# A vision-tower kernel on one core: dense FFN for all tokens one to two groups behind the load, chosen rows written by an indirect store

## The chip, the cores and the metric

The kernel runs on one NeuronCore of a Trainium2 chip. Its time is the device time in microseconds of one execution. Five engines work beside each other, each in the order of its own instruction list, and wait for each other through semaphores: TensorE (PE, with its weight loads PEld), VectorE (DVE), ScalarE (ACT), GpSimd (POOL) and SyncE (SP), which here only issues DMAs.

## The reference, cut to what matters

The input is 64 images of 12 channels and 224 x 224 pixels; the output is 64 x 196 tokens of 192 values.

```python
# tokens: sums over 16x16 patches, then a 12 -> 192 projection
pooled = x.reshape(B, 12, 14, 16, 14, 16).sum(axis=(3, 5))
h = einsum('bcij,ce->bije', pooled, channel_weights).reshape(B, 196, 192)
# attention on xn = layernorm(h): 12 heads of 16, causal softmax over 196 tokens
attn_output = ctx @ out_w + out_b
selection = softmax((xn @ sel_w + sel_b) / temperature)[..., 1:]
idx = top_k(selection[..., 0], 14)            # 14 of 196 tokens of each image
y = xn with (attn_output * selection) added in the rows idx
h = h + y
# FFN: 192 -> 768 with exact gelu -> 192
h = h + gelu(layernorm(h) @ in_weight.T + in_bias) @ out_weight
```

Only the 14 chosen tokens of an image get an attention output. All other tokens are a function of 12 channel sums and two rsqrt scales, so their layer norms and the first FFN layer can be computed from 13 numbers per token.

## The kernel before

**Tiling.** Images are worked on in 16 groups (NG) of 4 (GB). The input of a group comes in 7 tiles (XT) of 1344 KB into four buffers X. GpSimd adds row pairs of a tile (line 364, in place), VectorE reduces the rest (line 828, `sum_tile`) into R. When a group's seven tiles are done, SyncE stores R to a scratch in HBM (line 334) and reads it back in another layout (Praw, line 341), GpSimd adds the quarters (`sum_quarters`, lines 376 to 382) and so has P, the 48 channel sums x 196 tokens.

**Stages of a group.** A (tokens): TensorE multiplies P by TMR (`tm`, line 445), giving moments and features F; VectorE gets the variance and, by an integer guess and three Newton steps, its rsqrt (`rsqrt`, lines 831 to 851, one call a period for all norms: ln1 of one group, ln2 of another, the chosen rows' of a third). z is transposed (`zt`, line 451) to FM; the selection goes through an exponential and a top-14 search (`top`) on 4 rows, and `slots` builds the one-hot Sg, `keep` (not chosen) and ST, a one-hot that spreads the 56 chosen rows of a group over its 784 tokens (line 939). K (stacks): the 13 numbers of each token are split in bf16 parts (SP; H, M, L on ScalarE, d1, d2 on VectorE) and transposed (`tr1`, `tr2`) to Stk1 for the first FFN layer and Stk2 for the residual; `keep` zeroes the chosen tokens. G and S: the attention of the 56 chosen rows (SLOTS), two heads side by side (112 rows, six pairs): U (line 493), scores (508), maximum (988), six exponentials (647), twelve transposes to ET (514), context (520) with ET stationary and F moving, GN (996) normalised, transposed back (`gt`, 526), G2, output `at` (531), h1. C: the chosen rows' own layer norm and FFN (XH, `f1` line 546, actS, `f2` line 551) to OS. F1: dense first layer, twelve bf16 matmuls (line 560) through one PSUM bank psF, each followed by a gelu on ScalarE (line 669). F2: seven output tiles of 112 tokens, each six f32 products with W2 (line 573; the trace has two records for one f32 matmul), one with the residual stack (577) and one that adds the chosen rows by ST (581), then a copy to obuf (677) and one store of the group.

**Order.** Each engine runs a body per period p; every stage has a lag: A works on group p-1, attention on p-2 and p-3, stacks on p-2, F1 on p-3, F2 on p-4. The body of TensorE has 24 slots (lines 585 to 605): `AT_F1` names the slots with a first-layer matmul and `IN_F2` how many of the 56 matmuls of F2 follow in each, so that F1's wait for gelu and the waits for VectorE have output tiles of an older group beside them. ScalarE has the matching list (line 684) and VectorE an explicit one (line 1042) in which the seven tile reductions L0 to L6 are spread:

```python
plan = ["S gt 3", "C os 4", "L 0", "S at 3", "G ga 2", "L 1", "L 2", "G u 2", "L 3", "L 4", "A var 1", "R", "A z 1",
        "C xh 3", "S sc 2", "A sel 1", "K v 2", "L 5", "A top 1", "K d1 2", "L 6", "A slots 1", "S g 2", "K d2 2",
        "A var2 1"]
```

SyncE issues the load of a tile's buffer when VectorE has reduced the tile four earlier. All weights are loaded by SyncE (lines 304 to 324) between the first input tiles, and their products are built on VectorE and TensorE (`weights`, `prepare`) during the first two periods; TensorE enters its periods after that.

## Time and profile before

| | |
|---|---|
| median of 3 runs | 1011.47 us (1010.99 to 1015.18) |
| span of the profiled execution | 1015.8 us |
| TensorE busy | 851.5 us, 84%; its weight loads 727.0 us |
| VectorE busy | 603.5 us, 59% |
| ScalarE busy | 309.6 us, 30%; 96 exponentials of 446 ns |
| GpSimd busy | 366.9 us, 36%; 112 halvings of 3035 ns |
| tile reductions on VectorE | 112 of 1540 ns |
| mean granted TensorE clock | 0.840 of full speed |
| HBM | 159 MB read, 12 MB written, 168 GB/s over the span |
| dense store of a group | 588 KB, 9.0 us from issue to landing |
| sums to HBM, sums back | 147 KB each, 4.4 and 4.5 us |

A duration is that of one instruction or of a run of like ones. A line with a bracket tells how long the engine had been idle and what released it. The granted clock has two levels here, 1.00 (2.4 GHz) and 0.50 (1.2 GHz); numbers between are a window with both.

### The profile page before, as it was taken

The page shows a single profiled execution, that of the slowest core. Times are in us where ns is not written, and L with a number is a line of the kernel's source. Part 1 is how long each engine was busy: PE and PEld are TensorE (multiplying, and loading weights), DVE is VectorE, ACT ScalarE, POOL GpSimd, SP SyncE. Part 2 cuts the span into 40 slices and gives each one's busy share as a digit, 9 for nine tenths or more (in the row PEclk, how much of TensorE's full clock was granted, in tenths as well). Part 3 has the DMA queues.
Part 4 walks back from the last instruction along what each step waited for, and adds up shares of the span by engine and source line. Part 5 has one row for each costly group of instructions (what it writes and reads, how often), then busy time and mean ns, then how long its engine had stood idle before and what let it go on. Part 6 is the DMA issues. An engine that isn't in the chain of part 4 may idle for free.

```text
span 1015.8 us, 14313 instructions
## 1 busy us (share of the span) xinstructions
PE 851.5 (84%) x4772; PEld 727.0 (72%) x4772; DVE 603.5 (59%) x1305; ACT 309.6 (30%) x736; POOL 366.9 (36%) x164
## 2 busy tenths in 40 slices
PE   0550436499889999998989999999999999999998
PEld 0530334488678878887878888787888788889887
DVE  1769787856687777575665667474756555243200
ACT  0000023323234343333342424133333334253520
POOL 3484544434352626262624334262626240000000
PEclk9955555579899999796969789797979597999999
DMA  9674935444555565554646444455546441000000
GB/s 258 274 282 163 349 121 217 163 145 189 193 217 199 217 206 212 200 217 147 272 145 245 161 159 181 145 216 201 219 155 262 145 164 37 1 25 1 24 25 24
DMA packets 23901, 172.11 MB, mean 169 GB/s; under 512 B 3144, under 2 KB 6408, under 8 KB 9482
## 3 DMA queue, kind: packets, MB, share of 16 engines
q1 hardware_dynamic: 21770, 161.43, 43.5%
q10 hardware_dynamic: 2048, 9.63, 2.5%
q8 instruction: 44, 0.72, 0.3%
q14 instruction: 39, 0.32, 0.1%
HBM read 159.02 MB, written 12.04 MB: 168 GB/s over the span
## 4 chain that ended last, share of the span: by engine, by line
PE 64%; DVE 24%; ACT 4%; issue 3%; DMA 2%; SPq 1%; POOL 1%; DVEq 0%; POOLq 0%
PE psO L573 20%; PE psS L520 6%; PE psC L546 6%; PE psO L581 5%; PE psC L551 4%; PE psF L560 4%; PE psS L531 4%; DVE rx L880 3%; ACT Sm L647 3%; PE psS L514 3%; DVE ra L845 2%; PE psS L493 2%; DVE ry L841 2%; DVE mx L988 2%; DVE Sm L984 2%
## 5 line engine op out<-in xcount | busy, mean ns | idle before, releaser
L364 POOL TENSOR_TENSOR X<-X 128x1344 f32<-128x1344 f32 x112 | 339.7, 3035 | 464.5 <-DMA X<-in_x 463.9
L573 PE MATMUL psO<-W,act 128*112 128x192 f32 x1344 | 328.2, 383 | 1.1 <-ACT act L669 0.6
L573 PEld LDWEIGHTS psO<-W,act 128*112 128x112 f32 x1344 | 295.6, 296 | 14.7 <-issue 8.2
L828 DVE TENSOR_REDUCE R<-X 128x42 f32<-128x1344 f32 x112 | 170.4, 1540 | 14.9 <-POOL X L364 14.8
L669 ACT ACTIVATE act<-psF 128x392 f32<-128x392 f32 x192 | 95.3, 497 | 240.9 <-PE psF L560 240.8
L581 PE MATMUL psO<-OS,ST 56*112 56x192 f32 x224 | 81.7, 446 | 5.7 <-DVE OS L1026 5.7
L677 ACT ACTIVATE obuf<-psO 112x192 f32<-112x192 f32 x112 | 36.5, 326 | 129.2 <-PE psO L581 129.2
L560 PE MATMUL psF<-Stk,M1S 104*128 104x392 bf16 x192 | 69.5, 362 | 3.4 <-ACT act L669 3.4
L581 PEld LDWEIGHTS psO<-OS,ST 56*112 56x112 f32 x224 | 53.3, 284 | 17.4 <-DVE OS L1026 6.2
L520 PEld LDWEIGHTS psS<-F,ET 98*112 98x112 f32 x384 | 61.2, 256 | 2.0 <-ACT ET L654 1.9
L520 PE MATMUL psS<-F,ET 98*112 98x64 f32 x384 | 60.6, 340 | 1.5 <-ACT ET L654 1.5
L546 PE MATMUL psC<-XH,W1T 96*128 96x56 f32 (+1 forms) x384 | 59.5, 327 | 0.0
L546 PEld LDWEIGHTS psC<-XH,W1T 96*128 96x128 f32 (+1 forms) x384 | 59.0, 244 | 0.2 <-issue 0.2
L934 DVE TENSOR_TENSOR Sg<-psA,K 98x112 f32<-98x112 f32 x32 | 7.3, 268 | 85.8 <-PE psA L462 85.8
L874 DVE COPY F<-psA 98x216 f32<-98x216 f32 x16 | 6.1, 381 | 85.1 <-PE psA L445 85.1
L551 PE MATMUL psC<-W,actS 128*56 128x192 f32 x192 | 52.4, 446 | 0.0
L647 ACT ACTIVATE Sm<-Sm,nm 112x196 f32<-112x196 f32 x96 | 42.6, 446 | 28.9 <-DVE nm L990 28.9
L614 ACT ACTIVATE Ex<-Dm 98x16 f32<-98x16 f32 x16 | 3.5, 216 | 149.8 <-DVE Dm L889 149.8
L560 PEld LDWEIGHTS psF<-Stk,M1S 104*128 104x128 bf16 x192 | 23.4, 122 | 34.3 <-issue 27.1
L451 PE MATMUL psA<-K,F 98*64 98x98 f32 x32 | 6.0, 276 | 49.4 <-DVE lr L884 49.4
L551 PEld LDWEIGHTS psC<-W,actS 128*56 128x56 f32 x192 | 32.7, 179 | 16.3 <-issue 4.5
L531 PE MATMUL psS<-B,G 128*56 128x192 f32 x192 | 38.4, 355 | 3.2 <-DVE G L1002 3.2
(193 smaller groups left out, 1144.0 us busy)
## 6 DMA issues: line engine op xcount, KB each, us to landing
X<-in_x SPq DMA_DIRECT2D x112, 1344.0 KB, 7.7
out<-obuf ACTq DMA_DIRECT2D x16, 588.0 KB, 9.0
patch_sums<-R SPq DMA_DIRECT2D x16, 147.0 KB, 4.4
Praw<-patch_sums SPq DMA_DIRECT2D x16, 147.0 KB, 4.5
W1T<-in_w1t SPq DMA_DIRECT2D x1, 576.0 KB
W<-in_w SPq DMA_DIRECT2D x1, 576.0 KB
K<-in_consts SPq DMA_DIRECT2D x1, 480.5 KB
act<-in_wqkv SPq DMA_DIRECT2D x1, 432.0 KB
```

What stands on the lines that cost most here:

```text
L364: pool.tensor_tensor(v[:, :, 0:2, :], v[:, :, 0:2, :], v[:, :, 2:4, :], ALU.add).then_inc(pool_L.sem, 1)
L520: mm = pe.matmul(psS[0:ROWS, 0, j * ZR:(j + 1) * ZR], ET[:, k * HP + j, :], F[r][:, k, 0:ZR], start=(k == 0), stop=(k == 1))
L531: mm = pe.matmul(psS[0:SLOTS, 0, 0:D], G2[:, j, :], B2[:, j, :], start=(j == 0), stop=(j == HP - 1))
L546: mm = pe.matmul(psC[:, h * SLOTS:(h + 1) * SLOTS], W1T[rows, k, h * 128:(h + 1) * 128], XH[rows, k, :], start=(k == 0), stop=(k == 1))
L551: mm = pe.matmul(psC[0:SLOTS, 0:D], actS[:, h, :], W2[:, h, :], start=(h == 0), stop=(h == HT - 1))
L560: pe.matmul(psF[:, 0:GT // 2], M1S[:, (n // 2) * 128:(n // 2 + 1) * 128], Stk1[u % 2][:, (n % 2) * (GT // 2):(n % 2 + 1) * (GT // 2)], sta ...
L573: pe.matmul(to, tile_of(act_sb[u % 2][:, m, :], i), W2[:, m, :], start=(m == 0), stop=False)
L581: pe.matmul(to, tile_of(ST[u][:, :, :].rearrange("p b t -> p (b t)"), i), OS[u % 2][:, :], start=False, stop=True).then_inc(pe_F2.sem, 1)
L647: act.activation(Sm[:, j, :], Sm[:, j, :], ACT.Exp, bias=nm[:, j:j + 1], accum_out=rsum[:, j:j + 1]).then_inc(act_S.sem, 1)
L669: act.activation(act_sb[u % 2][:, n // 2, (n % 2) * (GT // 2):(n % 2 + 1) * (GT // 2)], psF[:, 0:GT // 2], ACT.Gelu).then_inc(act_F1.sem, 1)
L677: act.activation(obuf[u % 2][:, i, :], psO[(i + u) % 2][0:OT, 0:D], ACT.Copy).then_inc(act_F2.sem, 1)
L828: dve.tensor_reduce(R[:, u % 2, k * TQ * N:(k + 1) * TQ * N].rearrange("p (q j) -> p q j", q=TQ), v[:, :, :, 0:2, :], AX.XY, ALU.add).then ...
```

## The change

Stages and arithmetic are as before but for these:

- **Lags.** A, K, F1 and output tiles O0 to O2 work on the group loaded last (p-1); G too; attention S, tiles O3 to O6 and C on the one before it (p-2). Output tile 6 is taken apart into seven matmuls, one after each of the first seven matmuls of F1; the six of `at` come in pairs after later ones.
- **Dense FFN for all tokens.** `keep` goes: the chosen tokens' dense result is computed and stored too. ST, its matmul per output tile and the matmul with e4 go.
- **Indirect store.** VectorE computes the row numbers of the 56 chosen tokens (idx), and GpSimd writes OS over those rows of the output with an indirect DMA, after the group's dense store has landed (`store_chosen`). It does so in every second period, for two groups, between two halvings.
- **Chosen rows' FFN once for two groups.** h1 of two groups lies side by side (rows 0 and 64); stage C runs in every second period with 112 columns, its first layer in two parts (fa, fb) with a gelu each.
- **Tokens stationary in attention.** The exponentials are normalised on ScalarE (six Copy activations with a scale, `n`) before their transposes; the context product has F stationary and 336 columns of ET moving (four f32 matmuls for twelve) and comes out transposed, so GN and `gt` go.
- **rsqrt.** One call each for ln1 (in var), ln2 (in var2), both in each period, and for the chosen rows in every second, in place of one for all.
- **VectorE** reduces tiles two ahead of the others (AHEAD), and its reductions stand in new places.
- **Weights** are issued by ScalarE on its own queue, in three lots (channel weights and constants, FFN, attention); the M and R parts are built before the attention products.

```diff
+            def after_tile(i, c):
+
+                if c % XT == XT - 1:
+                    g, r = 4 * i + c // XT, (c // XT) % 2
+                    sp.wait_ge(dve_L, 4 * XT * i + c + 1)
+                    sp.dma_start(scratch[bass.ds(g, 1)].rearrange("o p q -> (o p) q"), R[:, r, :]).then_inc(sums_out[r], 16)
+                if not isinstance(i, int) or c + NX < NT:
+                    sp.wait_ge(dve_L, 4 * XT * i + c + 1)
+                    load_x(i, c + NX)
+                if c % XT == XT - 1:
+                    sp.wait_ge(sums_out[r], landed(g, r))
+                    if exists(g - 2):
+                        sp.wait_ge(pool_P.sem, pool_P.at(g - 2, "q23"))
+                    sp.dma_start(Praw[:, r, :], sums_in[bass.ds(g, 1)].rearrange("o p q -> (o p) q")).then_inc(sums_back[r], 16)
...
+            def store_chosen(g, k, e, q):
+
+                pool.wait_ge(dve_C.sem, dve_C.at(q, f"os{e}"))
+                pool.wait_ge(y_out[e], landed(g, e))
+                by_itself(pool)
+                pool.indirect_dma_start(orows, bass.IndirectOffsetOnAxis(ap=idx[k % 4][:, 0:1], axis=0), OS[e][:, :], None
+                                        ).then_inc(scat[e], 16)
...
+                    if s == 1 and k % 2 == 0:
+                        for e in range(2):
+                            g = 4 * i + k - 4 + e
+                            if active(g):
+                                store_chosen(g, k + e, e, 2 * i + k // 2 - 2)
+                g = 4 * i + k
+                if active(g):
+                    sum_quarters(g, k % 2)
...
+                    for i in range(2):
                         for k in range(2):
-                            mm = pe.matmul(psS[0:ROWS, 0, j * ZR:(j + 1) * ZR], ET[:, k * HP + j, :], F[r][:, k, 0:ZR],
+                            mm = pe.matmul(psS[0:ZR, 1 + i, 0:3 * ROWS], F[r][:, k, 0:ZR],
+                                           ET[:, k * HP + 3 * i:k * HP + 3 * i + 3, :].rearrange("p j s -> p (j s)"),
                                            start=(k == 0), stop=(k == 1))
...
+                elif name in ("fa", "fb"):
+                    pe.wait_ge(act_C.sem, act_C.at(q, "XH" if name == "fa" else "ga"))
+                    for h in range(HA) if name == "fa" else range(HA, HT):
+                        for k in range(2):
+                            mm = pe.matmul(psC[:, (h % HA) * ROWS:(h % HA + 1) * ROWS], W1T[bias_first(k), k, h * 128:(h + 1) * 128],
+                                           XH[bias_first(k), k, :], start=(k == 0), stop=(k == 1))
...
-                elif m == HT:
+                else:
                     if i == 0:
                         pe.wait_ge(act_K.sem, act_K.at(g, "k2"))
-                    pe.matmul(to, tile_of(Stk2[u][:, :], i), RS[:, :], start=False, stop=False)
...
+                    pe.matmul(to, tile_of(Stk2[u % 2][:, :], i), RS[:, :], start=False, stop=True).then_inc(pe_F2.sem, 1)
...
-                    pe.matmul(to, tile_of(ST[u][:, :, :].rearrange("p b t -> p (b t)"), i), OS[u % 2][:, :],
-                              start=False, stop=True).then_inc(pe_F2.sem, 1)
...
-            plan = {0: ["S gt 3"], 2: ["S at 3"], 3: ["K tr1 3"], 4: ["G ga 2"], 5: ["G u 2"], 6: ["K tr2 3"], 11: ["A tm 1"],
-                    13: ["S sc 2"], 16: ["A zt 1", "C xt 3"], 18: ["A sl 1"], 20: ["S et 2", "C f1 3"], 22: ["S g 2", "A st 1"],
-                    23: ["C f2 3"]}
...
+            plan = ("A:tm:1 S:sc:2 O:3:2 A:zt:1 O:4:2 O:5:2 S:et:2 K:tr1:1 S:g:2 K:tr2:1 "
+                    "f:0:1 o:6.0:2 f:1:1 o:6.1:2 f:2:1 o:6.2:2 f:3:1 o:6.3:2 f:4:1 o:6.4:2 f:5:1 o:6.5:2 f:6:1 o:6.6:2 A:sl:1 "
+                    "f:7:1 at:0:2 at:1:2 f:8:1 at:2:2 at:3:2 f:9:1 at:4:2 at:5:2 f:10:1 f:11:1 "
+                    "O:0:1 A:st:1 O:1:1 G:ga:1 C:xt:2 C:fa:2 G:u:1 O:2:1 C:fb:2 C:f2:2").split()
...
+                    act.wait_ge(dve_S.sem, dve_S.at(g, "ri"))
                     for j in range(HP):
-                        act.activation(Sm[:, j, :], Sm[:, j, :], ACT.Exp, bias=nm[:, j:j + 1],
-                                       accum_out=rsum[:, j:j + 1]).then_inc(act_S.sem, 1)
+                        act.activation(Sm[:, j, :], Sm[:, j, :], ACT.Copy, scale=rinv[:, j:j + 1]).then_inc(act_S.sem, 1)
...
-            plan = {0: ["K L 3"], 3: ["K k1 3"], 5: ["G rs 2"], 6: ["K k2 3"], 15: ["A e 1"], 16: ["A fm 1", "C XH 3"], 17: ["S exp 2"],
-                    19: ["K H 2"], 20: ["S t 2"], 21: ["C ge 3"], 22: ["K M 2"]}
...
+            plan = ("O:3:2 A:fm:1 S:e0:2 S:e1:2 S:e2:2 O:4:2 S:e3:2 S:e4:2 S:e5:2 A:e:1 O:5:2 K:H:1 S:n:2 K:M:1 S:t:2 K:L:1 K:k1:1 K:k2:1 "
+                    "f:0:1 f:1:1 f:2:1 f:3:1 f:4:1 f:5:1 f:6:1 O:6:2 f:7:1 f:8:1 f:9:1 f:10:1 f:11:1 "
+                    "O:0:1 O:1:1 C:XH:2 C:ga:2 G:rs:1 O:2:1 C:gb:2").split()
...
+                    dve.wait_ge(dve_A.sem, dve_A.at(g, "v2"))
+                    rsqrt(g, dve_R2, n2)
...
-                    dve.tensor_scalar(keep[:, :], col, 0.0, None, ALU.is_equal).then_inc(dve_A.sem, 1)
-                    dve.scalar_tensor_tensor(out=ST[u][:, :, :], in0=psA[0:SLOTS, 0:T].unsqueeze(1).broadcast_to([SLOTS, GB, T]),
-                                             scalar=kc("r1", SLOTS), in1=kc("bmt", SLOTS).unsqueeze(2).broadcast_to([SLOTS, GB, T]),
-                                             op0=ALU.is_equal, op1=ALU.mult).then_inc(dve_A.sem, 1)
...
+            plan = ("L:0:0 A:var:1 S:sc:2 A:log:1 L:1:0 A:var2:1 K:v:1 S:ri:2 L:2:0 K:d1:1 A:sel:1 L:3:0 K:d2:1 S:g:2 A:top:1 "
+                    "L:4:0 S:at:2 A:slots:1 C:xh:2 L:5:0 G:ga:1 L:6:0 G:u:1 C:os:2").split()
```

## Rows read from the trace of the kernel before

**Rows 1.** The engines, from part 1 of the page

```profile
PE 851.5 (84%) x4772; PEld 727.0 (72%) x4772; DVE 603.5 (59%) x1305; ACT 309.6 (30%) x736; POOL 366.9 (36%) x164
```

**Rows 2.** The chain that ended last: start us, us, what

```profile
231.72 2.02 PE psO L573 x10
...
337.10 2.02 PE psO L573 x10
...
386.31 2.02 PE psO L573 x10
...
879.48 2.02 PE psO L573 x10
```

**Rows 3.** Windows: busy us (instructions) of each engine, PEclk, DMA share, GB/s

```profile
350.00:400.00 50.00, 47.32 (x288) 40.53 (x287) 36.98 (x81) 19.34 (x46) 22.84 (x10) 0.97 0.57 212
...
516.00:518.00 2.00, 1.04 (x8) 1.04 (x9) 1.70 (x5) 1.32 (x7) 0.00 (x0) 0.88 0.00 0
518.00:520.00 2.00, 2.00 (x13) 2.00 (x11) 1.70 (x7) 1.46 (x4) 0.00 (x0) 0.50 0.97 226
...
536.00:538.00 2.00, 2.00 (x11) 2.00 (x11) 1.94 (x4) 0.00 (x0) 0.00 (x0) 1.00 0.00 0
```

**Rows 4.** Timeline of TensorE: start us, us, line, operation, count; chosen rows' FFN

```profile
310.70 2.80 PE L546 MATMUL psC<-XH,W1T 97*128 97x56 f32 x24
...
317.09 2.16 PE L551 MATMUL psC<-W,actS 128*56 128x192 f32 x12
...
518.75 5.23 PE L546 MATMUL psC<-XH,W1T 97*128 97x56 f32 x24
```

**Rows 5.** Timeline of VectorE from the moments' copy to the score maximum

```profile
341.66 0.38 DVE L874 COPY F<-psA 98x216 f32<-98x216 f32 x1 [6.31 <-PE psA L445]
...
343.20 2.80 DVE L880 TENSOR_SCALAR rx<-var 98x8 f32<-98x8 f32 x1
...
346.32 2.90 DVE L845 TENSOR_TENSOR ra<-ry 98x17 f32<-98x17 f32 x1
...
350.96 0.26 DVE L882 TENSOR_TENSOR F<-F,ry 98x96 f32<-98x96 f32 x1
...
351.98 1.37 DVE L984 TENSOR_TENSOR Sm<-psS,RM 112x1176 f32<-112x1176 f32 x1
...
354.79 0.17 DVE L990 TENSOR_SCALAR nm<-mx 112x6 f32<-112x6 f32 x1
```

**Rows 6.** Timeline of GpSimd in the same stretch

```profile
342.94 3.02 POOL L364 TENSOR_TENSOR X<-X 128x1344 f32<-128x1344 f32 x1 [0.18 <-DMA X<-in_x]
346.16 3.03 POOL L364 TENSOR_TENSOR X<-X 128x1344 f32<-128x1344 f32 x1 [0.19 <-DMA X<-in_x]
```

**Rows 7.** Line 845, an rsqrt step: ns min/median/max, first, last start

```profile
L845 DVE TENSOR_TENSOR ra<-ry x54: 177/178/2975, 90.3 to 960.3; 98x17 f32<-98x17 f32 x54
```

**Rows 8.** Timeline of TensorE near the end, at the full clock

```profile
986.34 0.34 PE L560 MATMUL psF<-Stk,M1S 104*128 104x392 bf16 x1
987.26 2.76 PE L573 MATMUL psO<-W,act 128*112 128x192 f32 x12 [0.59 <-ACT act L669]
...
990.05 0.72 PE L581 MATMUL psO<-OS,ST 56*112 56x192 f32 x2
990.70 2.76 PE L573 MATMUL psO<-W,act 128*112 128x192 f32 x12
```

**Rows 9.** Timeline of ScalarE: copies of ET and a table load

```profile
359.28 1.41 ACT L654 ACTIVATE ET<-psS 98x448 f32<-98x448 f32 x3
360.71 1.28 ACT L664 ACT_TABLE_LOAD   x1
```

**Rows 10.** Timeline of TensorE: the twelve heads' U

```profile
329.24 1.60 PE L493 MATMUL psS<-ZY,A 64*64 64x56 f32 x24
```

**Rows 11.** Part 6 of the page: input loads, median us to landing

```profile
X<-in_x SPq DMA_DIRECT2D x112, 1344.0 KB, 7.7
```

**Rows 12.** Timeline of TensorE: the first matmul of the moments

```profile
74.12 1.00 PE L445 MATMUL psA<-TMR,P 49*98 49x108 f32 x4 [9.87 <-POOL P L382]
```

684 lines of the change are left out of this document (348 added, 336 removed).

## The prediction

> **What bounds the kernel now.** I read the engines' busy time first: TensorE is busy 84% of 1015.8 us and no other engine is above 59% [rows 1]. Then the chain that ended last: from the first tile of the second-layer FFN to the end of the loads one period takes 54.0 us on average (231.72 to 879.48 us, twelve intervals), but one of them took 49.2 us (337.10 to 386.31) [rows 2]. The windows of 2 us tell why they differ: at 516 us the granted clock falls from 1.00 to 0.50, is 0.50 at 518 us, and is 1.00 again at 536 us [rows 3]; in that stretch the chosen rows' first layer takes 5.23 us, where it takes 2.80 us at the full level [rows 4]. Ahead of the fall TensorE waited for small VectorE steps: 1.04 us busy of 2 in the window in which it fell [rows 3]. So the kernel is TensorE work, some waits of 1 to 3 us, and half-speed stretches that follow them. Those VectorE steps are long for a reason too: from the copy of the moments at 341.66 to the end of the rsqrt and the product at 350.96 are 9.3 us, and 5.7 of them are two tiny steps of 2.80 and 2.90 us [rows 5], each of which ends where GpSimd's halving of a tile ends (342.94 + 3.02, 346.16 + 3.03) [rows 6]. The same step takes 0.18 us at its median and 2.98 at most [rows 7].
>
> **What leaves TensorE.** (a) ST and its matmul per output tile: a tile takes 987.26 to 990.70, 3.44 us, of which the ST pair holds 0.65 (990.05 to 990.70) [rows 8]. Seven tiles: 4.6 us a group, and a tile is 2.79. (b) The e4 matmul and the six GN transposes, each between 0.5 and 0.8 us by the neighbouring short pieces: 1.2 together. (c) The chosen rows' FFN once for two groups: now 2.80 + 2.16 [rows 4] and 0.3 for the transposes, 5.2 a group. With 112 columns in place of 56 the first layer is bounded by 2.8 (nothing more) and 5.6 (all doubled); I take 3.2, since 56 columns were short beside a 128-column weight load, so about 5.8 per pair: 2.3 a group saved. (d) Tokens stationary in the context product: 4 matmuls of 336 columns for 12 of 64, between 1.9 and 2.8 us, I take 2.2, no change. Sum: 8.1 us a group, 130 us over 16 groups, if TensorE's work still set the time. It also brings six ScalarE normalisations (under 2 us) and two further rsqrt chains in VectorE.
>
> **What order the change gives.** Before, attention, stacks and FFN ran two to four groups behind, so a step's inputs were mostly there. Now one group's tokens, stack, first FFN layer and three output tiles lie in one period. I walk one period, zero at the matmul of the moments, at the full clock and with no GpSimd stall. VectorE comes from C os and a tile reduction (1.54 us by the page) in one parity. From 2.3: copy, products, rsqrt, z take 9.3 - 5.7 = 3.7 [rows 5], to 6.0; scores, maximum, negation 3.0 (351.98 to 354.96) [rows 5], to 9.0; log 0.75 and a tile 1.5, to 11.3; var2 with its own rsqrt 2.9, to 14.2; stack and reciprocal 0.9, to 15.1. ScalarE has done the six exponentials beside it (446 ns each by the page) and now does H and six normalisations, 2.2, to 17.3. TensorE is through tm, scores, z transpose and three tiles at about 12.5: it **waits 4.8 us**. Transposes 1.2, copies of ET 1.4 [rows 9], L 0.5: 20.6; TensorE waits another 2.0 there. tr1, context, tr2: 3.3, to 23.9. Copy k2 0.8, then the gelu table, 1.28 [rows 9], first gelu 0.5: 26.5, another wait of 2.0. First layer: one PSUM bank, so each of twelve matmuls waits for the gelu before. A round took 0.92 us at the full level (986.34 to 987.26) [rows 8]; eleven rounds and a copy give 37. TensorE has 7.3 us of work to interleave there in 11. Then three tiles 8.4, st 0.45, ga 0.9, u 1.6 [rows 10], row sum 0.35 and 0.25 waiting for ZY: **49.0 us**. The other parity starts VectorE 1.7 us earlier, but xt waits for slots and the third rsqrt chain (3.4 us behind st), and fa, fb, gelu and f2 add the rest: 53.9. Mean **51.5 us**. TensorE's work is 47.32 of 50 us in the fast stretch from 350 us [rows 3], so 46.6 of 49.2 us now and 38.5 after: 75% of it.
>
> **GpSimd's lock.** The ops that stalled are those of rows 5 and 7. A period has seven halvings of 3.03 us as before [rows 6], and loads land 7.7 us after issue [rows 11], so the halvings released by the last tile reductions fall on the var, log and var2 stretch, and the queue that has waited for C os lets two go one behind the other. Now 5.7 us are lost in one period on that stretch; the new order has it twice and on TensorE's path. Bounds 0 (all in gaps) and 9 (three); I take 5.0: 56.5 us. The Trainium skill, "SBUF — State Buffer", section "Who interferes with whom", says that a VectorE instruction with two SBUF inputs or in a two-port mode shuts out, or waits for, a GpSimd instruction that reads SBUF, and that a reduction never does. The trace agrees with the first by 2.98 against 0.18 us in rows 7. By that rule three chains in place of one put more instructions at risk, which speaks against this change.
>
> **The clock.** A wait of 1 to 3 us was followed by about 17 us at 0.50 [rows 3]. Now there are 12 us of waits in each period and more with the stalls. At half, the transposes, context and tr cost 3.5 more, the attention output pairs among the first-layer matmuls and the rounds themselves 3.5, and if it lasts into the dense tiles O0 to O2, 3 to 8 more. Bounds 0 and 17. I take 8, a little above the 4.8 by which the mean period now exceeds the 49.2 us one, since the waits are more than twice as long: **64.5 us**.
>
> **Start and end.** The first moments matmul is at 74.1 us [rows 12]. Weights on ScalarE's queue no longer wait behind SyncE's, and the heads and A4, B2 come last; VectorE's 20 us of weight work and the trip through HBM stay: 60 to 78, I take 68. First period: no attention, 50. Fifteen full periods. Last: attention, chosen FFN, then the indirect store, which no row shows; nearest is the dense store, 9.0 us from issue to landing by the page, and the sums' 4.5. Below it can't gain, because it is behind os; I take 6, so the last stretch is 40. Where it isn't last it lies behind two periods of slack. Sum: 68 + 50 + 15 x 64.5 + 40 = 1125.5 in a profiled execution. That execution's span is 4.3 us above the median shown of 1011.5, so **1120 us**. The loads don't bound it: 7 x 3.03 us of halving and 1.7 of sums are 23 of 64.5. The page of the skill "SBUF — State Buffer", same section, also says that a DMA issued by GpSimd has its descriptors written through the shared port and is starved by two-port VectorE instructions; by that the last store could be some 3 us later, 1123. No row shows it.
>
> **Rivals.** (1) TensorE stays the bound: the waits named are filled by neighbouring work. For it: 84% busy now and 8.1 us less a group. Then 54.0 - 8.1 = 46 us a period: 68 + 45 + 15 x 46 + 35 = 838, and with half the new waits uncovered, about 900. Against it: engines run in order and I find nothing queued that could fill them. Chance 0.10. (2) The faster side: the chain as walked, but clock or stalls cost almost nothing. With no clock cost the first and last stretch are 8 shorter too: 150 + 15 x 56.5 - 4 = 993; with neither, 150 + 15 x 51.5 - 4 = 918. Mechanism: the dense run from O0 to O5, some 25 us, raises the clock, and it falls only where TensorE has slack. It decides from about 57 us a period: below that the kernel is faster, above slower. Chance 0.18. (3) The same, with the two costs summing to some 5.5 us: 1006 to 1017, no change: 0.05. (4) The clock stays low through the dense tiles as well, or the waiting indirect store holds GpSimd back so that halvings bunch: 72 us a period, 158 + 15 x 72 - 4 = 1234. Chance 0.08. (5) Forecast, 0.59, own range 1040 to 1200.
>
> **How the numbers follow.** A measurement of this kernel can tell 0.5% from no change. Faster: 0.10 + 0.18 = 0.28. Same 0.05. Slower: 0.59 + 0.08 = 0.67. Range: rival 1 and the lowest part of 2 stay out below (about 0.12), part of rival 4 above (0.06): 945 to 1205.
>
> **What would show it.** Starts of tm on average 64 us apart; TensorE idle ahead of the Sm transposes for 4 us or more on ScalarE's normalisations; a wait ahead of tr1, and one at the first-layer matmuls on act; the granted clock at 0.5 for over a third of each period; busy share of TensorE near 70%; tiny VectorE steps of 3 us in both rsqrt chains; no wait of TensorE on the loads' sums. Wrong if periods are under 57 us, if the clock stays above 0.85, or if the first tm is later than 80.

## The result, and the profile after the change

The changed kernel takes 1198.9 us (median of 4, 1184.27 to 1216.2), the kernel before beside it 1013.33 us (1010.99 to 1017.75): **1.171 times as long**, 95% interval 1.163 to 1.179. The profiled execution has a span of 1190.0 us and a mean granted clock of 0.764 (before: 1015.8 us and 0.840). Every ratio here is taken over the fast runs of both kernels (of the changed kernel 1184.27 and 1191.79 us), so it isn't the quotient of the medians, and the profiled executions of g1, g2 and e6 below are slow ones, 1.6 to 1.8% above their fastest. The forecast was 1120 us, so the direction and the range held and the size was 79 us short.

Part 1 of the page after, against [rows 1]:

```profile
PE 791.7 (67%) x3860; PEld 619.3 (52%) x3860; DVE 672.2 (56%) x1468; ACT 351.5 (30%) x826; POOL 379.0 (32%) x180
```

TensorE is busy 60 us less in spite of a lower clock, and VectorE 69 us more. The chain that ended last, by engine (part 4 of the page), first before, then after:

```profile
PE 64%; DVE 24%; ACT 4%; issue 3%; DMA 2%; SPq 1%; POOL 1%; DVEq 0%; POOLq 0%
```

```profile
PE 38%; DVE 35%; ACT 10%; issue 9%; DMA 4%; POOL 2%; ACTq 1%; DVEq 0%; POOLq 0%; SPq 0%
```

No engine is busy for more than 67% of the span any more, and TensorE holds 38% of the chain that ended last in place of 64%. What bounds the kernel now is the order of the work; the experiments below bear that out. The waits of TensorE after (the view of waits: us in total, times, longest) say where:

```profile
PE psA L438 <- DVE F L892: 125.4, 14, 10.9
...
PE psS L500 <- ACT Sm L658: 65.0, 16, 5.6
...
PE psF L543 <- ACT act L680: 54.3, 74, 2.4
...
PE psA L460 <- ACT SP L630: 47.5, 16, 16.6
```

The second to fourth are the three waits that the prediction's walk had: for the normalised exponentials, for the stack ahead of tr1, for the first gelu. The first, at the transpose of z, the walk did not have: there VectorE is late with its first rsqrt. Why, the timelines of VectorE and GpSimd show at one of the periods (start us, us, ..., idle before and releaser):

```profile
548.26 0.26 DVE L885 TENSOR_TENSOR prod<-F 98x96 f32<-98x96 f32 x1
...
548.84 9.15 DVE L889 TENSOR_SCALAR x_ln<-var 98x8 f32<-98x8 f32 x1
```

```profile
546.82 0.93 POOL L350 DMA_INDIRECT out<-OS,idx  x1 [8.69 <-DVE OS L1039]
548.05 0.91 POOL L350 DMA_INDIRECT out<-OS,idx  x1 [0.30 <-issue]
548.99 8.95 POOL L327 TENSOR_TENSOR X<-X 128x1344 f32<-128x1344 f32 x3
```

A scaling of 98x8 numbers, 177 ns when the halvings are cut small (e1, below), takes 9.15 us: it ends at 557.99, and three halvings that GpSimd runs back to back end at 557.94. They are back to back, with no wait for a load before any of them, because they had been ready while GpSimd stood 8.69 us in the wait ahead of the indirect store. In the next period the same happens at the product (line 885), after GpSimd's wait for the sums from HBM:

```profile
609.85 10.12 DVE L885 TENSOR_TENSOR prod<-F 98x96 f32<-98x96 f32 x1
```

```profile
603.15 0.54 POOL L336 TENSOR_TENSOR Pt<-Praw 48x196 f32<-48x196 f32 x1 [23.86 <-DMA Praw<-patch_sums]
...
604.92 14.93 POOL L327 TENSOR_TENSOR X<-X 128x1344 f32<-128x1344 f32 x5
```

GpSimd's two waits in all, and the four steps of VectorE that pay for them (groups by line: us in all, mean ns of one):

```profile
POOL Pt L336 <- DMA Praw<-patch_sums: 401.6, 16, 43.2
...
POOL out L350 <- DVE OS L1039: 158.8, 8, 89.7
```

```profile
L885 DVE TENSOR_TENSOR prod<-F 98x96 f32<-98x96 f32 x16 | 72.9, 4559 | 0.6
...
L889 DVE TENSOR_SCALAR x_ln<-var 98x8 f32<-98x8 f32 x16 | 50.3, 3143 | 0.5
...
L975 DVE TENSOR_SCALAR RM<-K,psS 112x196 f32<-112x196 f32 x16 | 23.2, 1447 | 0.0
...
L969 DVE TENSOR_TENSOR d<-d,SP 98x208 f32<-98x208 f32 x16 | 22.5, 1407 | 1.8 <-ACT SP L630 1.8
```

The mechanism is that of [rows 5] to [rows 7]; new is its length, and that one step is held through several halvings. In the kernel before it was not so. Its one run of four halvings let a step of VectorE in at the end of each of them:

```profile
123.35 11.96 POOL L364 TENSOR_TENSOR X<-X 128x1344 f32<-128x1344 f32 x4
```

```profile
126.81 2.58 DVE L880 TENSOR_SCALAR rx<-var 98x8 f32<-98x8 f32 x1
129.43 2.94 DVE L840 TENSOR_SCALAR rh<-rx 98x17 f32<-98x17 f32 x1
```

The clock is the last part. The context product with the tokens stationary, at 576.24 us after (timeline of TensorE):

```profile
575.39 0.93 PE L460 MATMUL psA<-identb,SP 98*104 98x98 bf16 x8 [2.07 <-ACT SP L630]
576.24 4.27 PE L506 MATMUL psS<-ET,F 98*64 98x336 f32 x8
```

In all sixteen groups it took 4.2 to 4.7 us, right behind the waits for ScalarE; it takes 2.48 us at the full level (f1, below).

### The profile page after: what moved, and what is told of

It is laid out like the page before. It is cut to its first block, busy times and chain, and to the rows that moved or that the text cites. A ratio compares the mean times of both kernels' runs of the same rounds, so it can differ in the third digit from the quotient of the medians.

```text
span 1190.0 us, 12432 instructions
## 1 busy us (share of the span) xinstructions
PE 791.7 (67%) x3860; PEld 619.3 (52%) x3860; DVE 672.2 (56%) x1468; ACT 351.5 (30%) x826; POOL 379.0 (32%) x180
## 4 chain that ended last, share of the span: by engine, by line
PE 38%; DVE 35%; ACT 10%; issue 9%; DMA 4%; POOL 2%; ACTq 1%; DVEq 0%; POOLq 0%; SPq 0%
PE psO L555 12%; DVE prod L885 6%; PE psS L506 6%; PE psF L543 5%; DVE x_ln L889 4%; DVE R L843 4%; ACT act L680 3%; ACT Sm L658 2%; PE psC L530 2%; PE psS L500 2%; DVE a_ln L853 2%; PE psA L460 2%; DVE mx L1000 2%; DVE Sm L996 2%; PE psS L515 2%
## 5 line engine op out<-in xcount | busy, mean ns | idle before, releaser
L555 PE MATMUL psO<-W,act 128*112 128x192 f32 x1344 | 369.4, 428 | 9.4 <-ACT act L680 9.4
L555 PEld LDWEIGHTS psO<-W,act 128*112 128x112 f32 x1344 | 324.7, 300 | 28.9 <-ACT act L680 13.5
L843 DVE TENSOR_REDUCE R<-X 128x42 f32<-128x1344 f32 x112 | 172.2, 1538 | 26.5 <-POOL X L327 26.2
L336 POOL TENSOR_TENSOR Pt<-Praw 48x196 f32<-48x196 f32 x16 | 8.6, 538 | 401.6 <-DMA Praw<-patch_sums 401.6
L438 PE MATMUL psA<-K,F 98*64 98x98 f32 x32 | 7.8, 343 | 130.8 <-DVE F L892 125.4
L1010 DVE TENSOR_TENSOR G<-psS,K 64x336 f32<-64x336 f32 x32 | 16.0, 500 | 113.8 <-PE psS L506 113.3
L500 PE MATMUL psS<-K,Sm 112*98 112x112 f32 x192 | 34.7, 359 | 65.0 <-ACT Sm L658 65.0
L506 PE MATMUL psS<-ET,F 98*64 98x336 f32 x128 | 72.6, 746 | 1.5 <-ACT ET L662 1.5
L885 DVE TENSOR_TENSOR prod<-F 98x96 f32<-98x96 f32 x16 | 72.9, 4559 | 0.6
L500 PEld LDWEIGHTS psS<-K,Sm 112*98 112x98 f32 x192 | 29.1, 179 | 67.6 <-ACT Sm L658 67.6
L460 PE MATMUL psA<-identb,SP 98*104 98x98 bf16 x256 | 27.0, 273 | 48.4 <-ACT SP L630 47.5
L460 PEld LDWEIGHTS psA<-identb,SP 98*104 98x104 bf16 x256 | 22.1, 181 | 66.6 <-issue 41.2
L889 DVE TENSOR_SCALAR x_ln<-var 98x8 f32<-98x8 f32 x16 | 50.3, 3143 | 0.5
```

Of the source, the lines that this page charges most:

```text
L460: mm = pe.transpose(to[0:SK, c0:c0 + HALF], SP[:, 2 * n + k, :, :].rearrange("p n c -> p (n c)"), identb[0:HALF, 0:HALF])
L500: mm = pe.transpose(psS[0:HALF, n // 4, (n % 4) * ROWS:(n % 4 + 1) * ROWS], Sm[:, j, k * HALF:(k + 1) * HALF], kc("ident")[0:ROWS, 0:ROWS])
L506: mm = pe.matmul(psS[0:ZR, 1 + i, 0:3 * ROWS], F[r][:, k, 0:ZR], ET[:, k * HP + 3 * i:k * HP + 3 * i + 3, :].rearrange("p j s -> p (j s)") ...
L555: pe.matmul(to, tile_of(act_sb[u % 2][:, m, :], i), W2[:, m, :], start=(m == 0), stop=False)
L843: dve.tensor_reduce(R[:, r, t * TQ * N:(t + 1) * TQ * N].rearrange("p (q j) -> p q j", q=TQ), v[:, :, :, 0:2, :], AX.XY, ALU.add).then_inc ...
L885: dve.tensor_tensor(prod[:, :, :], f[:, :, PR:FR], f[:, :, FR:FR + BC], ALU.mult).then_inc(dve_A.sem, 1)
```

## Where the periods stand in each kernel

I cut every profiled execution at the starts of the moments' matmul `tm`: up to the first one, the 15 periods to the sixteenth, and from there to the end. "Stalls" is VectorE's busy time above that of the same kernel with GpSimd's halving cut small (480.8 us before, 481.6 us after), so it counts what halvings add to VectorE's instructions. "Ratio" is that of the timed runs to the kernel before on the same chip; the runs were made on several chips, so spans of different rows differ by that too. In the kernels before, the first two periods lack the work of older groups (b1: 35.0 and 39.7 us), which makes their mean period short and their rest long. From the fourth period on a period is 54.0 us in before, 48.1 in b1, 68.3 in after, 58.9 in e1 and 55.6 in f1.

| kernel | ratio | span | clock | first tm | a period | rest | stalls |
|---|---|---|---|---|---|---|---|
| before | 1 | 1015.8 | 0.840 | 74.1 | 53.95 | 132.4 | 122.7 |
| b1 before, small halving | 0.906 | 906.6 | 0.901 | 65.1 | 46.95 | 137.3 | 0 |
| b2 before, no ST matmul | 0.957 | 972.2 | 0.831 | 71.6 | 52.1 | 118.7 | 155.7 |
| g1 before, reductions moved | 0.955 | 981.3 | 0.870 | 72.1 | 51.5 | 137.4 | 108.8 |
| g2 g1 with OS earlier | 0.963 | 967.7 | 0.875 | 71.9 | 50.6 | 137.4 | 92.0 |
| after | 1.171 | 1190.0 | 0.764 | 79.3 | 67.5 | 97.6 | 190.6 |
| e1 after, small halving | 1.033 | 1033.5 | 0.789 | 62.7 | 58.0 | 100.3 | 0 |
| f1 e1 with waits filled | 0.970 | 993.0 | 0.887 | 62.9 | 55.6 | 96.7 | 2.0 |
| e2 after, short fills | 1.190 | 1188.3 | 0.785 | 79.5 | 67.4 | 97.9 | 185.0 |
| e3 after, GpSimd's order | 1.120 | 1121.8 | 0.779 | 76.6 | 63.1 | 99.1 | 116.7 |
| e5 e3 and other orders | 1.118 | 1133.6 | 0.785 | 76.3 | 63.8 | 100.4 | 95.0 |
| e6 store's half of e3 | 1.165 | 1172.5 | 0.755 | 80.1 | 66.1 | 100.3 | 167.9 |
| e7 quarters' half of e3 | 1.163 | 1159.7 | 0.765 | 76.7 | 65.6 | 99.1 | 151.7 |
| e8 e3, reductions moved | 1.167 | 1161.9 | 0.745 | 78.0 | 65.6 | 100.3 | 121.3 |

## The experiments

Theory L says that the lock (VectorE's small steps held by halvings) is the term that the forecast had too small; theory K that it is the half-speed clock; R, in the later ones, that what remains without stalls is the chain of dependencies itself.

**e1 and b1: both kernels without the lock.** GpSimd halves 24 of the 1344 elements of a tile, so the input's sums are incomplete and the halving takes almost no time; all waits stay. The edit of e1 is shown; that of b1 is the same at its own line.

```diff
-                pool.tensor_tensor(v[:, :, 0:2, :], v[:, :, 0:2, :], v[:, :, 2:4, :], ALU.add).then_inc(pool_L, 1)
+                pool.tensor_tensor(v[:, :, 0:2, 0:4], v[:, :, 0:2, 0:4], v[:, :, 2:4, 0:4], ALU.add).then_inc(pool_L, 1)
```

> The changed kernel with GpSimd's halving cut from 1344 to 24 elements a partition (the sums are left incomplete; every wait, load and VectorE instruction stays). Theory L (VectorE's small steps are shut out by runs of GpSimd halvings): in the changed kernel these steps hold about 10.8 us a period over their short form (4.3 on prod, 3.0 on x_ln, the rest on later ones), of which TensorE's wait ahead of the z transpose shows 7.8; expected 1190 less 16 x 10, about 1030, periods 57 us, the z transpose's wait under 1 us. Theory K (the half clock after the waits is the larger cost, as the prediction had it, 8 against 5 us): about 1110, granted clock still under 0.80. Theory C (the bare chain of latencies): 51.5 us a period would be left only if both were gone.

> The kernel before with the same cut of the halving (24 of 1344 elements; sums incomplete). There the stalled steps hold 7 us a period over their short form, but older groups' output tiles lie beside them. Theory L with cover: 2 to 4 us a period less, about 965, against about 10 in the changed kernel. If the stalls were on TensorE's path in full: 16 x 7, about 900. If fully covered: 1010.

e1: 1034.99 us, ratio 1.033 (1.025 to 1.041), on a chip where before has a median of 1001.47. Its product and scaling:

```profile
L885 DVE TENSOR_TENSOR prod<-F 98x96 f32<-98x96 f32 x16 | 4.2, 262 | 0.6
...
L889 DVE TENSOR_SCALAR x_ln<-var 98x8 f32<-98x8 f32 x16 | 2.8, 177 | 0.6
```

and of TensorE's waits the first is gone, the second is not:

```profile
PE psS L500 <- ACT Sm L658: 76.3, 16, 5.6
...
PE psA L438 <- DVE F L892: 6.8, 7, 1.1
```

So stalls cost the changed kernel 9.5 us a period and 16.6 us ahead of the first tm. Two smaller things are in this price and e1 doesn't part them from it: VectorE's waits for halved tiles fall from 26.2 to 6.0 us in all, at most 1.3 us a period, and the clock rises from 0.764 to 0.789. b1: 908.85 us, ratio 0.906 (0.896 to 0.915). The kernel before pays 7.0 us a period for the same thing (5.9 from the fourth period on), nearly in full on its path though TensorE is its busiest engine: the form of the expectation with cover, 965, is wrong, that of the full price, 900, nearly right. With the lock out of both, after stands to before as 1.033 to 0.906, 14% longer: **of the 174 us between the two spans 127 us remain without any stall, and only 47 us are added by the lock.**

**e2: fill TensorE's waits.** 31 matmuls of 128x64 in each period, into the PSUM bank psF that is free there, 18 ahead of the z transpose, 9 ahead of the Sm transposes, 4 ahead of tr1.

```diff
-            plan = ("A:tm:1 S:sc:2 O:3:2 A:zt:1 O:4:2 O:5:2 S:et:2 K:tr1:1 S:g:2 K:tr2:1 "
+            plan = ("A:tm:1 S:sc:2 O:3:2 Z:18:1 A:zt:1 O:4:2 O:5:2 Z:9:1 S:et:2 Z:4:1 K:tr1:1 S:g:2 K:tr2:1 "
...
+                    if stage == "Z":
+                        for _ in range(int(step)):
+                            pe.matmul(psF[:, 0:64], kc("ident"), kc("ident")[:, 0:64], start=True, stop=True)
```

> The changed kernel with 31 extra f32 matmuls a period (identity times 64 columns into the idle bank psF, results unused): 18 ahead of the z transpose, 9 ahead of the Sm transposes, 4 ahead of tr1, about 7, 3.5 and 1.5 us of work in waits that last 8 to 10, 4 and 2 us. Theory K: the granted clock rises from 0.76 to over 0.90 and a period loses 6 to 8 us: about 1085. Theory L: the clock rises but a period loses 2 to 3 us, since much of the slow stretch is beside waits for gelu: about 1150. If the extra work overshoots short waits it adds up to 2 us a period.

1190.79 us, ratio 1.190 (1.180 to 1.200), clock 0.785. Neither form of the expectation holds, that of K (1085) no more than that of L (1150). The fill was too short: at one z transpose the 18 matmuls covered 4.16 us of a 10 us wait and 6.04 us stayed idle, and the context product behind the other two fills still took 4.2 us or more in fifteen of sixteen groups. So the run doesn't tell what the full level would give; f1 repeats it with longer fills and without the lock.

**f1: e1 with its waits filled.** 24 and 9 such matmuls ahead of the Sm transposes and tr1, halving small as in e1 (sums incomplete).

```diff
-            plan = ("A:tm:1 S:sc:2 O:3:2 A:zt:1 O:4:2 O:5:2 S:et:2 K:tr1:1 S:g:2 K:tr2:1 "
+            plan = ("A:tm:1 S:sc:2 O:3:2 A:zt:1 O:4:2 O:5:2 Z:24:1 S:et:2 Z:9:1 K:tr1:1 S:g:2 K:tr2:1 "
```

> The changed kernel with the small halving (sums incomplete, as before) and 33 extra f32 matmuls a period in TensorE's two long waits, 24 ahead of the Sm transposes (about 5.5 us) and 9 ahead of tr1 (about 2 us). With the small halving alone a period took 58.0 us where the bare chain of the prediction sums to 51.5. Theory K: the half clock holds the other 6.5 us; filled, the granted clock goes from 0.79 to over 0.90 and the time from 1035 to about 960. Rival R (the chain is longer than summed, the clock lies beside waits): under 1% less, 1025 to 1035.

984.92 us, ratio 0.970 (0.962 to 0.979), clock 0.887 against 0.789. TensorE in one period:

```profile
457.92 5.50 PE L574 MATMUL psF<-K 128*128 128x64 f32 x48
463.65 1.36 PE L500 MATMUL psS<-K,Sm 112*98 112x112 f32 x12 [0.24 <-ACT Sm L661]
464.85 2.13 PE L574 MATMUL psF<-K 128*128 128x64 f32 x18
467.04 0.58 PE L460 MATMUL psA<-identb,SP 98*104 98x98 bf16 x8
467.55 2.48 PE L506 MATMUL psS<-ET,F 98*64 98x336 f32 x8
```

The fill takes the place of the wait and makes nothing come earlier, yet the context product behind it now takes 2.48 us and not 4.3, and a period 55.6 us and not 58.0. This is the share of the clock, 2.4 us a period for 0.098 of the mean clock (by the ratios, 63 us in all; by the spans, 40). The measured time lies between the two forms of the expectation, 960 and 1025 to 1035, so both theories have a part: K is real, but after it 8.6 us a period still lie between f1 and b1 in the table, 7.5 from the fourth period on, with PE idle or on fill work. Single periods near the full level show the same (windows from tm to tm: us, busy of TensorE, granted clock, DMA share, GB/s), first f1 with and without stage C, then b1:

```profile
390.82:445.99 55.17, 49.62 (x315) 0.97 0.56 203
561.53:612.45 50.92, 44.61 (x277) 0.97 0.57 200
```

```profile
192.40:237.59 45.19, 45.10 (x287) 1.00 0.65 235
```

In f1 7.6 us of the busy time are fill. Without the lock and at the full level the kernel before is as long as TensorE's work (45.1 of 45.2 us); the changed kernel isn't, although it has less of it. That is R.

**e3: GpSimd's order.** The quarters' sums behind the first halving of the next body, the indirect stores behind the fifth halving.

```diff
-                    if s == 1 and k % 2 == 0:
+                    if s == 0 and active(4 * i + k - 1):
+                        sum_quarters(4 * i + k - 1, (k - 1) % 2)
+                    if s == 4 and k % 2 == 0:
...
-                g = 4 * i + k
-                if active(g):
-                    sum_quarters(g, k % 2)
```

> The changed kernel with GpSimd's list reordered alone: the sums of the quarters after the first halving of the next period's body in place of ahead of it, and the indirect stores after its fifth halving in place of after its second, so that neither wait holds halvings back and they don't run three to five in a row on VectorE's variance. Theory L: 4 to 6 us less a period, about 1110, and prod and x_ln together under half of their 7.7 us. Theory K: within 1% of 1190.

1121.88 us, ratio 1.120 (1.111 to 1.130), three tenths of the excess (0.051 of 0.171) won back by where two waits stand on an engine that is busy 32%. The mean product falls to 0.93 us, the scaling to 0.66 us, the wait at the z transpose from 125.4 to 48.6 us.

**e6 and e7: its two halves**, the store alone and the quarters alone.

> The kernel after, with one half of the earlier edit of GpSimd's order: only the indirect stores stand behind the fifth halving of a body; the quarters' sums stay at its end. Both halves together gave 1.120 times the kernel before, the kernel after 1.171. Theory L (what matters is how many halvings stand ready behind GpSimd's waits and run back to back over VectorE's small steps): the store's waits are 159 us in 8 places, the quarters' 402 us in 16, so the store's share is the smaller one, a third: 1.154, about 1165 us. Rival: the store is the whole of it, since its wait stands right ahead of the variance: 1.12 to 1.13.

> The kernel after, with the other half: only the quarters' sums stand behind the first halving of the next body, the indirect stores stay where they were. Theory L: two thirds of the gain, 1.137, about 1150 us. Rival (the store's wait is the whole): no change, 1.165 to 1.175.

1.165 (1.153 to 1.176) and 1.163 (1.153 to 1.173): either alone wins hardly anything, both together 0.051. Neither form of the expectation holds, that of one third and two thirds no more than that of the store alone. The two lines of VectorE, first e6, then e7:

```profile
L885 DVE TENSOR_TENSOR prod<-F 98x96 f32<-98x96 f32 x16 | 66.3, 4143 | 0.6
...
L889 DVE TENSOR_SCALAR x_ln<-var 98x8 f32<-98x8 f32 x16 | 5.2, 327 | 0.5
```

```profile
L888 DVE TENSOR_SCALAR x_ln<-var 98x8 f32<-98x8 f32 x16 | 50.1, 3131 | 0.6
...
L884 DVE TENSOR_TENSOR prod<-F 98x96 f32<-98x96 f32 x16 | 11.2, 702 | 0.6
```

Each wait has a victim of its own: with the quarters left where they were the product is held, with the store left, the scaling. In e7 one timeline has it alone, with the store as the only wait ahead of the run of halvings:

```profile
524.65 0.93 POOL L350 DMA_INDIRECT out<-OS,idx  x1 [12.86 <-DVE OS L1038]
525.88 0.92 POOL L350 DMA_INDIRECT out<-OS,idx  x1 [0.30 <-issue]
526.83 8.96 POOL L327 TENSOR_TENSOR X<-X 128x1344 f32<-128x1344 f32 x3
```

```profile
526.58 9.24 DVE L888 TENSOR_SCALAR x_ln<-var 98x8 f32<-98x8 f32 x1
```

From e3 to e7 the scaling gains 39.5 us (10.6 to 50.1) and the span 37.9. The spans of e3, e7, e6 and after stand in the order of their stalls (116.7, 151.7, 167.9, 190.6), but e6 and e7 can't be told apart by their ratios. Why the parts don't add I can say only in part: in e6 the later store moves halvings onto RM (2609 ns a step, after 1447), a new victim.

**e5: the order on the other engines, on top of e3.** Scores ahead of the variance on VectorE, the reciprocal behind the log, the normalisation ahead of the stack copies on ScalarE, context ahead of tr1 on TensorE.

```diff
-"L:0:0 A:var:1 S:sc:2 A:log:1 L:1:0 A:var2:1 K:v:1 S:ri:2 L:2:0 ...
+"L:0:0 S:sc:2 A:var:1 A:log:1 S:ri:2 L:1:0 A:var2:1 K:v:1 L:2:0 ...
-... A:e:1 O:5:2 K:H:1 S:n:2 K:M:1 S:t:2 K:L:1 ...
+... A:e:1 S:n:2 O:5:2 S:t:2 K:H:1 K:M:1 K:L:1 ...
-... S:et:2 K:tr1:1 S:g:2 K:tr2:1 ...
+... S:et:2 S:g:2 K:tr1:1 K:tr2:1 ...
```

> The changed kernel with GpSimd's new order and a new order of VectorE as well: scores ahead of the variance (their two long instructions don't compete with GpSimd), reciprocal behind log; ScalarE normalises ahead of the stack's copies, TensorE takes the context product ahead of tr1. Theory of the chain: the wait ahead of the Sm transposes (5 us) goes, tr1 gets later by the scores' 3 us less what GpSimd blocked anyway; 2 to 4 us less a period than with GpSimd's order alone (1122): about 1080. Rival: VectorE's sum decides and nothing moves, 1115 to 1125.

1134.59 us, ratio 1.118 (1.108 to 1.128), no gain over e3, as the rival had it. The wait that I aimed at went, and one as large came:

```profile
PE psA L437 <- DVE lr L893: 107.3, 16, 8.5
...
DVE rinv L1004 <- ACT Sm L652: 90.1, 16, 5.8
...
PE psS L499 <- ACT Sm L657: 23.8, 16, 1.9
```

TensorE no longer waits for the exponentials (23.8 us; 84.0 in e3), but VectorE waits for them with the z transpose's inputs queued behind. Three engines each pass through the same steps in one period, and an exchange of places within it moves the wait and doesn't shorten the path. This speaks for R.

**b2: the kernel before without ST's matmul** (the chosen rows are not added), one piece of work taken from TensorE and nothing else.

```diff
-                    pe.matmul(to, tile_of(Stk2[u][:, :], i), RS[:, :], start=False, stop=False)
-                else:
                     if i == 0:
                         pe.wait_ge(dve_C.sem, dve_C.at(g, "os"))
-                    pe.matmul(to, tile_of(ST[u][:, :, :].rearrange("p b t -> p (b t)"), i), OS[u % 2][:, :],
-                              start=False, stop=True).then_inc(pe_F2.sem, 1)
+                    pe.matmul(to, tile_of(Stk2[u][:, :], i), RS[:, :], start=False, stop=True).then_inc(pe_F2.sem, 1)
```

> The kernel before without the matmul that spreads the chosen rows over each output tile (ST and OS are still made and waited for; the chosen tokens come out without their attention row and FFN). It takes 0.65 x 7 = 4.6 us of TensorE work a group. If TensorE's work sets the kernel before: 16 x 4.6, about 930. If the order of waits sets it, less: 970 or above.

970.92 us, ratio 0.957 (0.948 to 0.966). By [rows 8] it is 4.6 us a group, 74 us; some 43 came off. The rest turned up as waits (z transpose: 49.4 us before, here 89.8) and the clock fell from 0.840 to 0.831:

```profile
PE psA L451 <- DVE lr L881: 89.8, 14, 22.9
```

VectorE's stalls rose as well, from 122.7 to 155.7 us, so part of what is missing is the lock once more; the run doesn't part it from the order of the waits.

**g1: the kernel before with its reductions moved**, so that fewer halvings are released ahead of the variance; the output is complete.

```diff
-... "G u 2", "L 3", "L 4", "A var 1", "R", "A z 1",
-"C xh 3", "S sc 2", "A sel 1", "K v 2", "L 5", "A top 1", "K d1 2", "L 6", "A slots 1", "S g 2", "K d2 2", ...
+... "G u 2", "A var 1", "R", "A z 1",
+"C xh 3", "S sc 2", "L 3", "A sel 1", "K v 2", "L 4", "A top 1", "K d1 2", "L 5", "A slots 1", "S g 2", "K d2 2", "L 6", ...
```

> The kernel before with two of VectorE's seven tile reductions (L3, L4) moved from just ahead of the variance and rsqrt to behind the scores, so that the loads they release are halved by GpSimd later than the rsqrt. Theory L: of the 7 us of stalls a period, whose whole price was 6.2 us when the halving was cut, 2 to 4 go: about 950. Rival: the halvings that fall on the rsqrt were released by L1 and L2 and stay, or others take their place: within 1%, 1001.

976.82 us, ratio **0.955** (0.945 to 0.965): faster than both kernels. Two lines of [rows 5] in this kernel:

```profile
L880 DVE TENSOR_SCALAR rx<-var 98x8 f32<-98x8 f32 x16 | 10.0, 624 | 0.6
...
L845 DVE TENSOR_TENSOR ra<-ry 98x17 f32<-98x17 f32 x54 | 9.6, 178 | 1.9
```

(2130 and 432 ns in the kernel before). The sum of the stalls falls by 14 us only, the span by 34.5: most stalls have moved to steps that nobody waits for at once. TensorE's wait ahead of the z transpose shows it, 49.4 us before and 14.7 here. The edit also takes two reductions, 3.1 us of VectorE's own work, from ahead of the variance, but that isn't what gained: in the kernel before VectorE stood idle there already and waited for tm,

```profile
DVE F L874 <- PE psA L445: 85.1, 15, 9.9
```

and here it waits 120.5 us in the same place. From the moments' copy to the end of the rsqrt are 9.3 us in the mean before, 5.1 here and 3.4 in b1. Where a stall lies counts for more than how long it is.

**g2: g1 with the last addition of the chosen rows ahead of the second variance**, since g1's tiles waited 41.6 us for it.

```diff
-"S gt 3", "C os 4", "L 0", ... "K d2 2", "L 6", "A var2 1"
+"S gt 3", "L 0", ... "K d2 2", "L 6", "C os 3", "A var2 1"
```

> The kernel before with its reductions moved as in the version that gained 4.5%, and the chosen rows' last addition put at the end of the body, ahead of the second variance, where it stood behind the next body's first step. In that version TensorE's output tiles waited 42 us in 9 places for it. Theory: that wait falls below 10 us and half of it is gained: 0.955 minus 0.02 = 0.935, about 945 us. Rival: the wait only passes on to VectorE's queue, which now waits there for the matmuls of the second layer, and the variance comes later: 0.95 to 0.97.

965.37 us. That wait fell to 1.9 us, the ratio is 0.963 (0.953 to 0.974), against 0.955 for g1 with intervals that overlap: no gain is shown, and the expected 0.935 is outside.

**e8: the same remedy on the changed kernel** (with e3's order): no reduction ahead of the second stack copy.

```diff
-"L:0:0 A:var:1 S:sc:2 A:log:1 L:1:0 A:var2:1 K:v:1 S:ri:2 L:2:0 K:d1:1 A:sel:1 L:3:0 K:d2:1 S:g:2 A:top:1 "
-"L:4:0 S:at:2 A:slots:1 C:xh:2 L:5:0 G:ga:1 L:6:0 G:u:1 C:os:2"
+"A:var:1 S:sc:2 A:log:1 A:var2:1 K:v:1 S:ri:2 K:d1:1 L:0:0 A:sel:1 L:1:0 K:d2:1 S:g:2 A:top:1 "
+"L:2:0 L:3:0 S:at:2 A:slots:1 L:4:0 C:xh:2 G:ga:1 L:5:0 G:u:1 L:6:0 C:os:2"
```

> The kernel after with both edits of GpSimd's order, and VectorE's reductions taken out of the stretch of variance, scores and second variance (none before the second stack copy; then L0, L1, L2 and so on), as in the version of the kernel before that gained 4.5%. Theory L: a halving that is released by these reductions lands 6 us later, so with none released there the small steps go free, the chain ahead of the normalisations is 3 us shorter by the reductions themselves and some 3 us by the locks: 1.120 minus 16 x 5 / 1010 = 1.04, about 1050 us, with product and last scaling of the variance under 500 ns. Rival: the loads now run late in each period, GpSimd's backlog reaches the next period's start all the same, and the buffers come free later: 1.10 to 1.13.

1164.51 us, ratio 1.167 (1.157 to 1.176): the remedy costs 4% against e3, and the time is above both forms of the expectation. The last scaling of the variance is free (171 ns in the mean), but the product, expected under 500 ns, takes 4183 (934 in e3), 52 us more in all. The timelines of GpSimd and VectorE, and TensorE's wait:

```profile
591.72 0.59 POOL L343 TENSOR_TENSOR P<-Pt 48x196 f32<-48x196 f32 x1 [0.17 <-POOL Pt L337]
592.27 8.98 POOL L327 TENSOR_TENSOR X<-X 128x1344 f32<-128x1344 f32 x3
```

```profile
593.93 7.43 DVE L884 TENSOR_TENSOR prod<-F 98x96 f32<-98x96 f32 x1
```

```profile
PE psA L431 <- POOL P L343: 19.3, 7, 4.8
```

At this place the last reduction comes so late that the period waits for P, and what makes P also lets three ready halvings go: tm starts at 592.45, its product at 593.93, inside them. In the changed kernel a group's moments are the first thing after its last tile; the kernel before has them late in the body. I take that to be the slack that g1 uses; no run tests it by itself.

## Why the prediction was right and wrong, step by step

**The table of the forecast against the trace**, in us of the profiled execution: first tm 68, measured 79.3; first period 50, measured 63.9; the following 14 periods 64.5 each, measured 67.8; the last period and the end 104.5, measured 97.6. The differences are +11.3, +13.9, +46.3 and -6.9, in sum 64.6 of the 64.5 us by which 1125.5 missed 1190.0.

**The walk of one period, 51.5 us: right within 2 us.** (Two of its sums are off by 0.1 and 0.2 us, 9.3 - 5.7 and 17.3 + 1.2 + 1.4 + 0.5, which changes nothing.) Its three waits were 4.8, 2.0 and 2.0 us; measured are 4.1 us (65.0 / 16; in e1 76.3 / 16 = 4.8), about 2.1 us (47.5 less the one of 16.6, over 15), and 2.16 us at the first gelu in the period shown. Without the lock a period is 58.0 at clock 0.789 and 55.6 at 0.887; continued by the same slope to 1.00 it is 52.8, an estimate from e1 and f1. The two periods of f1 at 0.97 shown above took 50.9 us without stage C and 55.2 with it, where the walk had 49.0 and 53.9. In after itself the last stretch behind the loads, where no halving is left, takes 50.5 us from the scores of one period to those of the next (no stage C between; the walk had 49.0 for that parity), in the timeline of TensorE:

```profile
1092.88 2.16 PE L494 MATMUL psS<-FM,UB 64*112 64x196 f32 x12
...
1143.41 2.24 PE L494 MATMUL psS<-FM,UB 64*112 64x196 f32 x12
```

So the core of the forecast, that the order and not the work sets the time, is shown by e1 (1.033 without any lock, although TensorE has less to do) and by f1 beside b1; e5 agrees with it.

**Work taken from TensorE: sizes right.** The context product takes 2.47 us in f1 at the full level and 2.48 us in the kernel before: no change, as forecast (2.2). The chosen rows' first layer in two parts takes 2.04 + 1.07 = 3.1 us, forecast 3.2. Busy time by mean clock falls from 715 to 605 us, roughly 6.9 us a group, forecast 8.1. Since the sum went by the chain, no credit was taken for it, and b2 shows that even in the kernel before only some 43 of 74 us came off.

**The lock: the step that failed.** The forecast took 5.0 us a period, bounds 0 and 9; e1 shows 58.0 against 67.5, 9.5, past the upper bound (8.2 at the least, if all the waits for halved tiles are taken off). Two things were wrong. The size: I priced a stall at one halving, 3 us, as in rows 5 to 7, and counted how many such there could be. In the changed kernel a held step waits for all that is left of a run of halvings, up to four of them. The price was that of the kernel before, and rightly read there: its run of four, at 123.35 us, let a step in at the end of each. So the traces of before could not have told me the length; e3 shows what it costs. The place: I let two halvings go in a row behind the wait for C os. The wait for the sums (401.6 us in all) I left out of the step, although sum_quarters had been moved from behind the fifth halving to the end of the body. Rival 4, "the waiting indirect store holds GpSimd back so that halvings bunch", at 0.08 and 72 us a period, had the mechanism; e3, e6 and e7 show it and its second half, the wait for the sums. I should have made it part of the forecast: the diff shows both waits. The same error is in the start: without stalls the first tm is at 62.7 us, low in my bounds, and 16.6 us of stalls bring it to 79.3. The last and largest of these stalls is one instruction of the weights:

```profile
73.61 5.60 DVE L806 SCALAR_TENSOR_TENSOR B<-OB,K,B 64x192 f32<-64x192 f32 x1
```

**The clock: too dear.** Forecast 8 us a period (0 to 17); from 58.0 to the 52.8 of the estimate are 5.2, of which f1 measured 2.4. The term is lower than the forecast's, within its bounds. Granted levels were as forecast (0.764 in the mean is 0.50 for almost half of the time). This error hides part of the lock's, which is luck: 52.8 + 5.2 + 9.5 = 67.5, forecast 51.5 + 8 + 5 = 64.5.

**The first period** was taken as free of attention and 50 us; it measured 63.9, in e1 50.5. Without stalls it was right. **The end**: 6 us for the indirect store behind `os`; `os` ends at 1185.18 and the execution at 1190.0, 4.8 us. The issue of one took 0.93 us of GpSimd. The starving of descriptors, by which the prediction had the last store some 3 us later, isn't seen in any run. What I didn't say is that the shorter lags save 35 us there (rest of 97.6 against 132.4), a gain of the change that the sum held without naming it.

**What would show it.** Right: waits at the transposes, tr1 and gelu, share of PE (67%), clock, no wait of TensorE for the loads' sums in after, 3 us and longer steps in the first rsqrt chain. Wrong: the second chain is hardly touched (its first step 349 ns in the mean).

**Rivals.** TensorE as the bound (838 to 900) is out: busy 67%, clearest in e1. The faster side needed periods below 57; none of the changed kernel's variants with full halvings comes under 63.1. But it is near: without lock and with its waits filled, f1 is 3% faster than the kernel before as it stands. It isn't faster than that kernel without its own lock (b1, 0.906).

**Open.** f1 and b1 have nearly the same clock (0.887 and 0.901), so the 7.5 to 8.6 us a period between them are chain almost alone; single periods at 0.97 and 1.00 show it, no run is at the full level throughout. What makes a run of halvings hold a step through in one kernel and not in the other is open. Whether an order for all engines exists in which the changed kernel's chain is short wasn't found; e5 tried one.

## What to carry to other kernels

Before groups are drawn together into one period, walk that period along all engines: work saved on the busiest engine was worth about half of itself here where waits and stalls took the rest (b2), and waits were paid again by the clock (f1). A wait in GpSimd's queue isn't free because GpSimd is idle two thirds of the time: what has become ready behind it runs in one piece, and the step of VectorE that comes just then can pay for the whole piece. Look for small VectorE instructions that are long in the trace, and move what releases the halvings, not the work; but only where the moved loads have slack (g1), not where the period starts with them (e8).
